# A fused attention and feed-forward layer: loads placed among the slots, low-rank products on 128 rows, a new order

## What is computed

```python
def attn(q, k, v):                 # q = layernorm(x); k = v = context
    q, k = rms_norm(q, q_norm_w), rms_norm(k, k_norm_w)
    q, k = rope(q), rope(k)        # 16 heads of 32, 4 key heads
    p = softmax(where(causal, q @ k.T / sqrt(32), -1e30))
    return (p @ v) @ w_out.T

def ffn(x1):
    w_up   = dequant4bit(w_up_q, w_up_scale).T       # 512 x 2048
    w_down = dequant4bit(w_down_q, w_down_scale).T   # 2048 x 512
    x2 = relu(x1 @ w_up + b_up + x1 @ w_up_lora_a @ w_up_lora_b)
    return x2 @ w_down + b_down + x2 @ w_down_lora_a @ w_down_lora_b

x = x + attn(layernorm(x), ctx, ctx)
x = x + ffn(layernorm(x))
```

## Time and profile before

| | us |
|---|---|
| median of 3 runs | 493.28 (492.91 to 493.85) |
| the profiled execution | 493.2 |
| its span, first to last instruction | 491.4 |
| TensorE busy | 444.3 (90%) |
| VectorE busy | 345.7 (70%) |
| ScalarE busy | 302.8 (62%) |
| GpSimd busy | 275.5 (56%) |
| mean granted TensorE clock | 0.985 of full |

### The profile page before, as it was taken

How to read it: one execution, slowest core, us unless ns; L and a number is a source line. 1 busy time by engine, 2 the same in 40 slices (tenths; PEclk the granted TensorE clock), 3 DMA queues, 4 the chain that set the end, 5 groups by cost and what they waited for, 6 DMA issues and landing times.

```text
span 491.4 us, 8266 instructions
## 1 busy us (share of the span) xinstructions
PE 444.3 (90%) x2416; PEld 214.7 (44%) x2416; DVE 345.7 (70%) x1075; ACT 302.8 (62%) x927; POOL 275.5 (56%) x308
## 2 busy tenths in 40 slices
PE   0155578999999999999999999999999999999997
PEld 0134434445454545454545454545454444444443
DVE  3959986995959695959595968686777766544341
...
GB/s 141 392 127 135 195 232 194 91 95 139 139 156 142 153 139 156 140 156 130 166 119 177 99 192 96 189 114 173 111 173 108 155 118 141 118 87 128 65 73 55
DMA packets 208140, 70.17 MB, mean 143 GB/s; under 512 B 197808, under 2 KB 200496, under 8 KB 207456
## 3 DMA queue, kind: packets, MB, share of 16 engines
...
q0 software_dynamic: 80, 0.16, 0.1%
...
## 4 chain that ended last, share of the span: by engine, by line
PE 85%; DVE 6%; DMA 3%; ACT 3%; issue 1%; SPq 0%; DVEq 0%; ACTq 0%
PE ff L919 34%; PE ff L933 34%; PE tb L901 8%; PE sb L873 3%; PE tb L889 2%; PE ff L778 2%; DMA wd_lo<-wd_hi 2%; DMA wd_hi<-in_L_xattn_k_norm_w 1%; DVE pr L1176 1%; PE ff L829 1%; ACT pr L675 1%; DVE big L1070 1%; DVE wu_lo L1078 1%; DVE t_sin L1144 0%; ACT wu_hi L632 0%
## 5 line engine op out<-in xcount | busy, mean ns | idle before, releaser
L919 PE MATMUL ff<-wu_hi,xnT 128*128 128x512 f16 x512 | 153.7, 382 | 0.0
L933 PE MATMUL ff<-wd_hi,x 128*128 128x512 f16 x512 | 152.3, 379 | 0.0
L492 POOL TENSOR_TENSOR pr<-pr,rinv 128x512 f32<-128x512 f32 x64 | 73.3, 1145 | 104.3 <-DVE rinv L1086 104.3
L675 ACT ACTIVATE pr<-pr,nmax 128x128 f32<-128x128 f32 x256 | 98.7, 387 | 1.9 <-DVE nmax L1176 1.9
L740 ACT ACTIVATE hid<-z 128x512 f16<-128x512 f32 x64 | 40.2, 628 | 94.6 <-DVE z L1107 94.5
L919 PE MATMUL ff<-wu_lo,xnT 128*128 128x512 f16 x256 | 97.5, 381 | 0.0
L933 PE MATMUL ff<-wd_lo,x 128*128 128x512 f16 x256 | 97.0, 379 | 0.0
L1176 DVE CUSTOM_DVE_ANT_0 pr<-sb,tabs,score_scale 128x128 f32<-128x128 f32 x256 | 73.6, 343 | 23.3 <-PE sb L873 23.2
L1107 DVE SCALAR_TENSOR_TENSOR z<-ff,su,b_row 128x512 f32<-128x512 f32 x64 | 47.8, 746 | 58.5 <-PE ff L919 57.4
L501 POOL TENSOR_TENSOR big<-pr,big 128x512 f16<-128x512 f32 x64 | 76.0, 1198 | 20.8 <-ACT big L706 20.8
L919 PEld LDWEIGHTS ff<-wu_hi,xnT 128*128 128x128 f16 x512 | 48.6, 99 | 59.8 <-issue 7.7
...
## 6 DMA issues: line engine op xcount, KB each, us to landing
...
big<-in_L_ffn_w_up_q SPq DMA_DIRECT2D x4, 1024.0 KB, 7.5
big<-in_L_ffn_w_down_q SPq DMA_DIRECT2D x4, 1024.0 KB, 5.8
...
wd_lo<-in_L_xattn_w_out SPq DMA_DIRECT2D x1, 1024.0 KB, 7.8
b_row<-in_L_ffn_b_up SPq DMA_DIRECT2D x1, 1024.0 KB, 15.3
pT<-big SPq DMA_TRANSPOSE x64, 3.4
```

The lines of the kernel that those rows point to most:

```text
L492: pool.tensor_tensor(pr[:, m], pr[:, m], rinv[:, p, 4 * m:4 * m + 4].unsqueeze(2).broadcast_to([P, NG, P]), ALU.mult).then_inc(probs, 1)
L675: last = act.activation(pr[:, m, g, :], pr[:, m, g, :], ACT.Exp, bias=nmax[:, p, j:j + 1], scale=-1.0, accum_out=rsum[:, p, j:j + 1])
L919: last = pe.matmul(bank[:], a[:, m, :], b[:, m, 512 * g:512 * g + 512], start=(m == 0 and i == 0), stop=(m == KC - 1 and i == 2))
L933: last = pe.matmul(ff[down_bank[n]][:], x2T[:, part, k + h % HG, :], b[:, h, :], start=(h == 0 and i == 0), stop=(h == HC - 1 and i == 2))
```

## The change

- New numbers in nearly all tables of the order; `PERIOD` stays. VectorE dequantizes 27 of the 32 tiles instead of 24, GpSimd 5 instead of 8.
- Of SyncE's loads only batch 0 and group 0 stay ahead of the slots. Batch 1, w_out and group 1 get slots, as do group 2, batch 2 and the bias row further back than before.
- The two norm weights have a semaphore each; their maxima are taken in `norm_powers`, after the other maxima; the statistics of batch 0 stand behind `gather_tops`. GpSimd builds the query's tables before those of the keys.
- ScalarE's loads start with the up scales, the mask and rotary tables come last. The down scales and the up product's A are laid out so that a partition reads one contiguous piece; the rows of the down weight are dealt to partitions by (p j) instead of (j p), and the turned part of a down tile is written to columns four apart, as that of an up tile is.
- The low-rank product of the down tiles reads 128 rows of both factors. GpSimd zeroes three more areas for it, and the waits for these go from 2 to 4.

```diff
-R_KTURN = (259, 483, 1126, 1637)
+R_KTURN = (414, 630, 1275, 1592)
-LOAD_AT = (3, 282, 526, 863, 944, 1212)
-ROW_LOAD_AT, DOWN_BIAS_LOAD_AT = 7, 1179
-BATCH_LOAD_AT = (2, 777)
+LOAD_AT = (369, 421, 557, 574, 1092, 1168, 1277)
+WO_LOAD_AT = 242
+ROW_LOAD_AT, DOWN_BIAS_LOAD_AT = 1233, 817
+BATCH_LOAD_AT = (106, 540, 1498)
...
-        a_dn3, a_dn3_late = sb("a_dn3", [R3, H // 2], F16), low_area[0:R3, 3584:4096].bitcast(F16)
+        a_dn3_all, a_dn3_late_all = sb("a_dn3", [P, H // 2], F16), low_area[:, 3584:4096].bitcast(F16)
+        a_dn3, a_dn3_late = a_dn3_all[0:R3], a_dn3_late_all[0:R3]
+        b_dn3_all = high_area[:, 3840:4096].bitcast(F16)
...
-        wdq_v = wdq.rearrange("(j p) (g c) -> g p j c", p=P, c=512)
+        wdq_v = wdq.rearrange("(p j) (g c) -> g p j c", p=P, c=512)
...
             load_batch(0)
             sp.wait_ge(lora_a_in, 16 * 3)
-            sp.wait_ge(norm_w_in, 16 * 2)
+            sp.wait_ge(k_weight_in, 16)
+            sp.wait_ge(q_weight_in, 16)
             load_group(0)
-            sp.dma_start(wo_raw, wo.rearrange("(j p) c -> p j c", p=P)).then_inc(wout_in, 16)
-            load_group(1)
-            load_batch(1)
...
+                if s == WO_LOAD_AT:
+                    sp.dma_start(wo_raw, wo.rearrange("(j p) c -> p j c", p=P)).then_inc(wout_in, 16)
...
-            pool.memset(high_area[:, 3584:3840], 0.0).then_inc(lora_rows_empty, 1)
+            pool.memset(high_area[:, 3584:4096], 0.0).then_inc(lora_rows_empty, 1)
             pool.memset(low_area[:, 2048:3072], 0.0).then_inc(lora_rows_empty, 1)
+            pool.memset(low_area[:, 3872:4096], 0.0).then_inc(lora_rows_empty, 1)
+            pool.memset(a_dn3_all[:], 0.0).then_inc(lora_rows_empty, 1)
...
-            act.dma_start(tabs[:], tabs_d).then_inc(consts_in, 16)
...
             act.dma_start(b_nat[:], bu.rearrange("(p a) -> p a", p=P)).then_inc(lora_a_in, 16)
+            act.dma_start(tabs[:], tabs_d).then_inc(consts_in, 16)
...
-                    a, b = (a_dn3[:], a_dn3_late)[t // 24][:, P * (t % 8):P * (t % 8) + P], b_dn3
+                    a, b = (a_dn3_all, a_dn3_late_all)[t // 24][:, P * (t % 8):P * (t % 8) + P], b_dn3_all
...
-                    cols = slice(i, None, 4) if t < UP_TILES else slice(P * i, P * i + P)
-                    last = turn(bank[:, cols], stage[:, g % W_RING, i, P * j:P * j + P],
+                    last = turn(bank[:, i::4], stage[:, g % W_RING, i, P * j:P * j + P],
...
-                dve.wait_ge(norm_w_in, 16 * 2)
-                for j, w in enumerate((qw_bc, kw_bc)):
-                    norm_link(dve.tensor_reduce(wmax[:, j:j + 1], w, AXX, ALU.max, apply_absolute_value=True), wait=False)
...
-                input_stats(0)
...
             def norm_powers():
+                dve.wait_ge(q_weight_in, 16)
+                dve.wait_ge(k_weight_in, 16)
+                for j, w in enumerate((qw_bc, kw_bc)):
+                    norm_link(dve.tensor_reduce(wmax[:, j:j + 1], w, AXX, ALU.max, apply_absolute_value=True), wait=False)
...
             gather_tops()
+            input_stats(0)
             norm_scales()
```

More of the change, by code:

```diff
@@ L68 @@
[L68 to L73 removed]
+R_STATS = (0, 8, 397, 1356)
+R_SQUARES = (2, 5, 556, 1555)
@@ new lines @@
+R_MOMENTS = (0, 23, 473, 1390)
+R_KEYS = (0, 5, 293, 1861)
+R_POW = (2, 4, 759, 1936)
+R_CENTRE = (3, 49, 653, 1683)
+R_SINES = (2, 100, 544, 1479)
+R_COSINES = (3, 17, 661, 2053)
+R_ROPE = (3, 194, 683, 1491)
+R_KSPLIT = (4, 171, 1051, 1721)
+R_KLOW = (22, 201, 1005, 1486)
+R_KTURN = (414, 630, 1275, 1592)
+R_QSPLIT = (13, 260, 982, 1760)
+R_QLOW = (7, 335, 965, 1506)
+R_QTURN = (399, 627, 1271, 1609)
+R_SCORES = ((53, 499, 1363, 1830), (165, 518, 1473, 1850), (190, 618, 1613, 1870), (255, 824, 1653, 1924))
@@ new lines @@
+R_PLOW = ((405, 1050, 2054, 2417), (446, 1059, 2191, 2455), (503, 1414, 2308, 2597), (522, 1534, 2367, 2615))
+R_PTURN = ((677, 1298, 1741, 1911), (724, 1385, 1757, 1995), (1040, 1422, 1772, 2056), (1046, 1479, 1788, 2070))
+R_VSUM = (466, 790, 1166, 1825)
+R_VARG = (451, 576, 1089, 1717)
+R_VPOW = (526, 688, 1127, 2391)
+R_VSPLIT = (701, 1333, 1813, 2183)
+R_VLOW = (629, 1498, 2199, 2631)
+R_PV = (832, 1586, 1929, 2266)
+R_OHIGH = (808, 1517, 2036, 2336)
+R_OLOW = (647, 1400, 1785, 2110)
+R_PROJ = (982, 1674, 2009, 2302)
@@ L103 @@
+LORA_TURN_AT = (2, 3, 4)
+LORA_COPY_AT = (16, 21, 166)
+WO_ORDER_AT = (45, 51, 52, 99)
+WO_TURN_AT = (183, 212, 363, 374)
+WO_HIGH_AT = (248, 347, 393, 417)
+WO_LOW_AT = (355, 356, 394, 398)
+LORA_A_AT, LORA_ALOW_AT = 6, 4
+BIAS_ROW_AT = (1081, 1180, 1374, 1450)
+WO_SQUARES_AT, WO_SUM_AT, WO_ARG_AT, WO_POW_AT = 41, 5, 83, 87
 RING, W_RING, HID_RING = 4, 3, 3
@@ L409, in _ @@
                         sp.dma_start_transpose(x2T[:, g], hid[:, (4 * n + g) % HID_RING].rearrange("p a h -> p (a h)")).then_inc(x2_turned[g], 16)
-                for g in range(2, 8):
-                    if LOAD_AT[g - 2] == s:
+                for g in range(1, 8):
+                    if LOAD_AT[g - 1] == s:
                         load_group(g)
```

134 lines of the change are left out of this document (49 added, 85 removed).

## The result

The changed kernel takes 485.72 us (median of 4 runs, 485.03 to 486.27), the kernel before 493.25 in the same session (492.91 to 493.85): a ratio of 0.9845, 95% interval 0.9828 to 0.9862. The prediction was 485.3 with a range of 480.0 to 491.0. The total is right; three of its terms are not, and their errors mostly cancel.

A forecast was written before the change was run, and what follows sets the result against it. TensorE's work was taken to bound the kernel from about 75.5 us, after a start with some 44 us of its idle; 493.2 - 4.8 (start) - 3.1 (rows) - 1.5 (clock) + 1.5 (waits) = 485.3 us, range 480.0 to 491.0.

The forecast's parts named there:

- What bounds it: Whole kernel: TensorE's work alone from about 75.5 us on, some 44 us of its idle before that.
- First turned part: At the start: fewer loads ahead of the B rows move it from 29.73 to 24.7, 5.0 us earlier.
- I take the scales as 0.3 us earlier: Ahead of B low: maxima no longer wait for norm weights, statistics move back, so the scales come 0.3 us earlier.
- What reaches tile 20: Up to 75.5 us: VectorE's 5.74 us wait goes, tile 20's release comes near 70.7; -4.8 us, bounds 0 and -6.
- the wait for group 2: VectorE a little after 31 us: group 2 lands late, costing 1.0 to 2.7 us, taken as 1.2.
- 128 rows: Twelve down tiles after 75.5 us: turned parts take 0.65 us instead of 0.91; -3.1 us.
- Clock and new waits: Behind tile 20: less half clock -1.5 us (bounds 0, -4.2); waits for VectorE +1.5 us (bounds 0, +5).
- Steady part: Later batches: same matmuls in another order, no new wait, 0 us.
- (a): Rival: earlier start given back to waits by 75.5 us, only the 128 rows remain; 490.1 us, chance 0.13.
- (b): Rival: whole gain at the start and no half clock after tile 20; 479.9 us, chance 0.12.
- (c): Rival: last x2 part late every batch, each us over 8.6 costs 13 us; 498.3 with 1 us, chance 0.08.
- (d): Rival: bias row lands late and ScalarE stands 3.8 us, 489, or 493 to 495 if later; late form chance 0.03.

The follow-up runs named there:

- b_loads: Kernel before, with only group 2, batch 2 and the bias row issued behind the B rows and both transposes of batch 0: 490.13 us.
- a_loads: Changed kernel, with group 2, batch 2 and the bias row issued ahead of the B rows again: 488.02 us.
- a_pool_max: Changed kernel, with GpSimd's table order of the kernel before and the two norm maxima ahead of the others again: 484.49 us.
- b_rows128: Kernel before, with only the low-rank product of the down tiles reading 128 rows of both factors: 489.45 us.
- b_cols: Kernel before, with only the down weight's rows dealt (p j) and down tiles' results written to columns four apart: 492.75 us.
- a_rows48: Changed kernel, with 48 rows back in the low-rank product of the down tiles: 487.34 us.

## Why the prediction was right, point by point

**What bounds it: right.** Saturated TensorE from tile 20 on and a sparse start. The steady 372.8 us are the same in both kernels.

**First turned part: predicted -5.0, measured -3.5.** The mechanism, loads ahead of the rows, is shown (b_loads -5.3, a_loads +2.7). The step that was mis-sized is "I take the scales as 0.3 us earlier": they came 1.56 us later (18.77 against 17.21 for the last scale). I had put the statistics behind the gathering and counted them as off the way, but VectorE has no gap between the maxima and `take_tops`: what is moved within one full list is still in front. `take_tops` comes 1.55 us later (15.23, before 13.68): the list starts 0.3 later, and three steps stood longer beside GpSimd (0.40, 1.19 and 0.41 us where 0.16, 0.40 and 0.14 stood before). a_pool_max gave back 1.27 of these 1.56 us, and the first turned part with them. The rows' landing was near: 4.0 us from the start of the issue to the last landing, 4.6 in the sum. The last 0.45 us are w_out's sum, which the working did not have ahead of the first turned part.

**What reaches tile 20: predicted -4.8, measured -3.7.** The wait of 5.74 us is gone, as predicted; the wait for group 2 is 0.48 and not 1.2, since it landed some 5 us after its issue at 27.73 and VectorE came to it late itself. By the rows from 17.5 us to tile 20, VectorE's idle time fell from 8.1 to 2.8 us, by 5.3 where the working has 4.5 (5.7 less 1.2), although it now holds 1.1 us of waits for ScalarE's high parts that the working did not have. Its busy time there rose from 49.9 to 51.6 us, where the working has it level: the scales' steps, done at 17.5 before, now run to 19.1. So the term fell short by the scales, -5.3 + 1.7 = -3.6, and not by anything behind them.

**128 rows: right as work, -3.1.** 0.65 us for each down tile, shown by b_rows128 and b_cols. Two rules were weighed. "TensorE: Matmul & The Clock Gate", section "Step-by-step: what each phase is for", in the Trainium skill says that the row count does not matter for a weight load. The traces agree for the load itself (0.10 us with 128 rows, 0.09 with 48); what failed is the reading that 48 rows then cost nothing (0.91 against 0.65), and by it the sum would have been 485.3 + 3.1 = 488.4, not the 488.1 of the prediction. "TensorEngine Tiling (Array Packing)", section "Key Properties", also in the Trainium skill, says that a change of the tiling mode drains TensorE, and not that a matmul of 48 rows is one; read so, the traces agree with it, since the extra time lies at the two changes of shape.

**Clock and new waits: each term wrong, their sum near.** By the clock of 1.00 in the rows behind tile 20 the clock term is -4.2 instead of -1.5, the bound; what is then left for the waits is 36.1 - (39.8 - 4.2 - 3.1) = +3.7 instead of +1.5, within the bound of 5. 1.87 of it stands as idle time in the rows. The rest is not seen directly; short waits that the modelled ends hide are one part: 90.87 follows 89.80 after 1.07 us where 0.22 are needed, and the row lists 0.69. That the total came within half a microsecond is in part luck: the start was 1.1 us short, and clock and waits together gave 0.5 more than the 0 booked for them. It is not luck alone. In the stretch behind tile 20 TensorE, at full clock and with 128 rows, needs what VectorE needs: VectorE is busy for 31.9 of 36.1 us there, and for 15.23 of 16 from 84 to 100. a_rows48 shows it from the other side: 3.1 us more TensorE work and a piece at half clock, and no idle time of TensorE at all. I treated two faces of one quantity as separate terms.

**Steady part: right, 0.** No wait of TensorE after 110 us.

**Rivals.** (a) did not come true; part of the start was lost ahead of tile 20, as described. (b) had the clock and the rows right, the start and the waits wrong. (c), the late x2 part, was not seen in any steady batch; one wait of 0.62 us stands at 105.28 in the first. (d): the bias row landed 9.2 us after its issue at 60.67, and nothing waited for it.
